# Projecting images 2 to 15 of a vision tower as two packed fp32r products instead of one fp32 product

## The chip, the cores and the metric

One core of one Trainium2 chip runs the whole kernel. The time is that of the device in microseconds, from several runs of the same program; the kernel before took 1002.57 us (median of 3 runs, 1000.47 to 1002.79). A further execution was taken with the hardware profiler: 1000.1 us, of which 998.5 us lie between the first and the last instruction. All rows of the trace are from that one.

## The reference, cut to what matters

Sixteen images of 256 tokens with 4 heads of 64 channels go through a token mixer, a gated recurrence with a residual, and a mixture of eight experts (top 2) with a shared expert. The change touches the first products:

```python
def proj(w, b):
    y = jnp.einsum('nclh,dc->ndlh', x, w) + b[None, :, None, None]
    return _flatten(y)
q, k, v = proj(Wq_w, Wq_b), proj(Wk_w, Wk_b), proj(Wv_w, Wv_b)
ek = jnp.exp(k)
num = jnp.einsum('ts,nsd->ntd', ew, ek * v)
den = jnp.einsum('ts,nsd->ntd', ew, ek)
y = jax.nn.sigmoid(q) * num / den
h = y @ out_w + out_b + _flatten(x)        # then layer norm, the recurrence, the experts
```

The host puts q, k, v and the residual with `out_b` side by side, so that one product with 256 columns per head gives all four.

## The kernel before

The kernel has two parts. The **mixer** takes the images one after another in a pipeline of steps t = 0 to 18: step t projects image t and forms its sums, works on the output, norm, gates and scan of image t-1, on the residual and norm of image t-2, and runs the shared expert and the routing for image t-3. Steps 0 to 3 and 16 to 18 are written out; steps 4 to 15 are a loop over pairs, whose body is `step` on each engine. The **experts** follow: 36 blocks of 256 routed rows.

Every engine runs its own written list of named pieces (`project0`, `hidden`, `gates0`, ...), and semaphores join them. Nothing is reordered at run time, so an engine that waits holds back all that stands behind it in its list. What the change and the steps of the prediction touch:

- TensorE: `project(n, par, lt)` makes one half (`lt`) of an image: four matmuls, one per head, with 128 tokens of x as the stationary operand (65 partitions: 64 channels and a row of ones for the bias; every fourth element, since the heads lie innermost) and 256 columns of `wproj` as the moving one, in fp32. In the trace each of these is two records of line 832, so eight records per half. The other large products already are fp32r with values split in a high and a low part: `split_product` (line 748) for `hidden`, `gates0/1`, `input0/1`, and `project_hidden` (line 764) for `ffn_out`.
- `project1` waits for `ekv0` of VectorE (the bank of PSUM is read by then), and `hidden(t, 0)` waits for `ekv1`, since it writes into the same banks.
- ScalarE: `exp_and_tanh` (lines 1299 to 1305) reads the projection three times; `copy_yt`, `copy_u`, `copy_v`, `gelu_j`, `high`, `tanh0/1` are the rest of its step.
- VectorE: `ekv` (1765), `h_sum`, `h_norm`, `u_stats`, `u_norm`, `v_sum`, `v_norm`, `ratio0/1` (reciprocals, 1772), `y_last`, `low` (the low parts for `ffn_out`, 1593), `gate_a/b`, the routing (`best`, `second`, `places`, `slots_out`), `base_sum` (1999).
- GpSimd: `inv_std` (517, 520) for three norms, `affine` (585, 587), `out_bias` (598), `rows_out` (four scattering DMAs, 524), and at two places the loading of a set of expert weights (`load_high`, `load_stage`, 4 MB) with the subtraction of its low parts (`split_low`, 510).
- SyncE: the loading of x, and the stores.
- Between the parts `block_limits` reads eight block limits on TensorE and ScalarE, and TensorE runs eight matmuls (line 1262) that produce nothing.

## Time and profile before

| what | us |
|---|---|
| median of 3 runs | 1002.57 |
| profiled execution | 1000.1 |
| its span | 998.5 |
| TensorE busy in it | 941.2 (94%) |
| VectorE, ScalarE, GpSimd busy | 676.5, 458.8, 380.1 |
| mixer, to the last product of the shared expert | about 543 |
| experts | about 445 |

Busy time of TensorE counts from a matmul's start to its modelled end; as matmuls overlap, the start-to-start distance is what one costs. The granted clock is given as a share of 2.4 GHz: 1.00 is 2.4 GHz throughout, 0.5 is 1.2 GHz. The mixer's steps are told apart by the transposes of Y with which each begins on TensorE (line 839): step 4 begins at 106.54 us and step 16 at 476.90 us.

### The profile page before, as it was taken

How to read it: one execution, taken by the hardware profiler on the slowest of the kernel's cores; microseconds unless marked ns; L12 is line 12 of the kernel's file. 1: busy time of each engine (PE TensorE's matmuls, PEld its weight loads, DVE VectorE, ACT ScalarE, POOL GpSimd, SP SyncE). 2: the span in 40 equal slices, each digit the busy share in tenths (PEclk: the TensorE clock that was granted, in tenths of full speed). 3: DMA queues.
4: the chain of work that ended last, by engine and by line, in shares of the span. 5: the costliest groups of instructions: out<-in, count | busy, mean ns of one | idle time of the engine just before them, and what ended most of it. 6: DMA issues, size and time to landing. Idle time of an engine off the chain costs nothing.

```text
span 998.5 us, 21487 instructions
## 1 busy us (share of the span) xinstructions
PE 941.2 (94%) x6801; PEld 879.6 (88%) x6801; DVE 676.5 (68%) x2092; ACT 458.8 (46%) x1132; POOL 380.1 (38%) x470
## 2 busy tenths in 40 slices
PE   6879999999999999999886999999999999999996
PEld 4667898888898888988786999999999999999995
DVE  3687878877888777788887365645656456554643
ACT  2214344444444434444332455555555555555553
POOL 5272533334324243233535334342423435342322
PEclk9989999999999999999999899999999999999998
DMA  9305111011110011100025727372463826474222
GB/s 271 134 18 168 43 43 37 17 32 42 42 42 16 26 42 42 42 21 11 33 95 195 202 47 204 55 216 43 101 157 50 215 47 145 117 174 92 43 43 32
DMA packets 49187, 84.84 MB, mean 85 GB/s; under 512 B 6415, under 2 KB 30881, under 8 KB 49154
## 3 DMA queue, kind: packets, MB, share of 16 engines
q0 software_dynamic: 31056, 57.46, 23.6%
q1 hardware_dynamic: 18098, 26.96, 9.2%
q8 instruction: 17, 0.28, 0.1%
q14 instruction: 16, 0.13, 0.0%
HBM read 55.34 MB, written 29.09 MB: 85 GB/s over the span
## 4 chain that ended last, share of the span: by engine, by line
PE 59%; issue 21%; POOL 9%; DVE 7%; ACT 1%; POOLq 1%; DMA 0%; DVEq 0%; SPq 0%; ACTq 0%
PE ps_nd L764 17%; PE ps_proj L748 13%; PE ps_ri L748 6%; PE ps_nd L925 6%; PE ps_proj L832 5%; POOL out L709 5%; PE ps_ip L748 4%; PE ps_h L913 2%; PE ps_t L839 2%; PE ps_ip L898 2%; PE ps_t L1234 1%; POOL v_rows L524 1%; DVE E L1765 1%; POOL rstd L520 1%; DVE yb L1999 1%
## 5 line engine op out<-in xcount | busy, mean ns | idle before, releaser
L1593 DVE TENSOR_TENSOR GL<-g_act,GH 128x256 fp32r<-128x256 f32 (+1 forms) x416 | 171.3, 425 | 166.4 <-ACT GH L1293 164.9
L1288 ACT ACTIVATE g_act<-ps_proj,fcb 128x256 f32<-128x256 f32 (+1 forms) x272 | 129.5, 476 | 277.9 <-PE ps_proj L748 253.4
L764 PE MATMUL ps_nd<-w2h,GH 128*128 128x256 f32 x832 | 240.6, 289 | 2.4 <-DVE GL L1593 2.2
L764 PE MATMUL ps_nd<-w2h,GL 128*128 128x256 f32 x832 | 233.8, 281 | 0.0
L764 PE MATMUL ps_nd<-w2l,GH 128*128 128x256 f32 x832 | 232.9, 280 | 0.0
L764 PEld LDWEIGHTS ps_nd<-w2h,GH 128*128 128x128 f32 x832 | 156.3, 188 | 6.9 <-issue 1.8
L1293 ACT CAST GH<-g_act 128x256 fp32r<-128x256 f32 (+1 forms) x416 | 161.0, 401 | 1.1
L764 PEld LDWEIGHTS ps_nd<-w2l,GH 128*128 128x128 f32 x832 | 157.0, 189 | 0.0
L764 PEld LDWEIGHTS ps_nd<-w2h,GL 128*128 128x128 f32 x832 | 156.4, 188 | 0.0
L748 PE MATMUL ps_proj<-xh,w1h 128*128 128x256 f32 (+1 forms) x544 | 126.8, 315 | 10.1 <-DVE E L1765 8.7
L709 POOL DMA_INDIRECT out<-yb,rows_to x72 | 115.6, 1605 | 16.7 <-issue 14.0
L748 PE MATMUL ps_proj<-xl,w1h 128*128 128x256 f32 (+1 forms) x544 | 111.8, 287 | 0.0
L748 PE MATMUL ps_proj<-xh,w1l 128*128 128x256 f32 (+1 forms) x544 | 111.3, 286 | 0.0
L748 PEld LDWEIGHTS ps_proj<-xh,w1h 128*128 128x128 f32 x544 | 86.7, 192 | 26.1 <-issue 14.3
L338 POOL TENSOR_TENSOR carrier_pool<-minus_half 1x1 f32<-1x1 f32 x48 | 10.9, 226 | 206.4 <-DVE slots L1987 113.9
L748 PEld LDWEIGHTS ps_proj<-xl,w1h 128*128 128x128 f32 x544 | 86.6, 194 | 0.0
L748 PEld LDWEIGHTS ps_proj<-xh,w1l 128*128 128x128 f32 x544 | 85.9, 193 | 0.0
L524 POOL DMA_INDIRECT v_rows<-v,slots x64 | 67.9, 1060 | 32.7 <-issue 16.6
L832 PE MATMUL ps_proj<-wproj,x 65*128 65x256 f32 x256 | 71.2, 425 | 6.8 <-DMA x<-x 6.2
L925 PE MATMUL ps_nd<-E,ewT 128*128 128x512 f32 x128 | 72.8, 702 | 2.8 <-DVE E L1765 2.8
L832 PEld LDWEIGHTS ps_proj<-wproj,x 65*128 65x128 f32 x256 | 64.1, 327 | 9.9 <-issue 7.9
L338 POOL TENSOR_TENSOR carrier_y<-minus_half 1x1 f32<-1x1 f32 x36 | 9.4, 261 | 162.8 <-DVE yb L2314 162.8
(266 smaller groups left out, 1829.9 us busy)
## 6 DMA issues: line engine op xcount, KB each, us to landing
R<-v_rows SPq DMA_DIRECT2D x37, 260.0 KB, 2.7
w1h<-fc_w POOLq DMA_DIRECT2D x9, 1024.0 KB
w2h<-pj_w POOLq DMA_DIRECT2D x9, 1024.0 KB
stage<-fc_w POOLq DMA_DIRECT2D x9, 1024.0 KB, 11.4
stage<-pj_w POOLq DMA_DIRECT2D x9, 1024.0 KB, 13.9
v_rows<-tail_rows SPq DMA_DIRECT2D x8, 520.0 KB, 4.5
x<-x SPq DMA_DIRECT2D x16, 256.0 KB, 3.5
out<-yb SPq DMA_DIRECT2D x16, 256.0 KB, 2.1
```

Of the source, the lines that this page charges most:

```text
L338: return pool.tensor_tensor(carrier[use][:], half, half, ALU.add)
L524: pool.indirect_dma_start(out=v_rows, out_offset=bass.IndirectOffsetOnAxis(ap=where_to, axis=0), in_=source, in_offset=None).then_inc(sema ...
L709: pool.indirect_dma_start(out=out, out_offset=bass.IndirectOffsetOnAxis(ap=rows_to[:, a:a + 1], axis=0), in_=yb[:, a, :], in_offset=None, ...
L748: last = pe.matmul(dst, w[a][:, k, cols], rhs, start=(q == 0), stop=(q == len(parts) - 1))
L764: last = pe.matmul(banks[a], g[:, j, a * P:(a + 1) * P], w[i][:, j, :], start=(j == 0 and q == 0), stop=(j == HT - 1 and q == 2))
L832: last = pe.matmul(ps_proj[:, h, :], head_view(par, lt, h), wproj[:, h, :], start=True, stop=True)
L839: last = pe.transpose(ps_t[:, f, lt * P:(lt + 1) * P], src[:, lt, f * P:(f + 1) * P], ident[:])
L898: last = pe.matmul(ps_ip[:, lt, :], HS[:, k, lt * P:(lt + 1) * P], wout_sb[:, k, :], start=(k == 0), stop=(k == FT - 1))
L925: last = pe.matmul(ps_nd[:, tt, :], ewT[:, s, tt * P:(tt + 1) * P], E[:, s, :], start=(s == 0), stop=(s == LT - 1))
L1288: act.activation(g_act[:, j % G_SLOTS, 0:width], banks[j % len(banks)][:, 0:width], ACT.Gelu_apprx_tanh, bias=fcb[i][:, j:j + 1]).then_inc ...
L1293: act.copy(GH[:, j, 0:width], g_act[:, j % G_SLOTS, 0:width]).then_inc(gh_done, 1)
L1593: dve.tensor_tensor(GL[:, j, 0:width], g_act[:, j % G_SLOTS, 0:width], GH[:, j, 0:width].bitcast(F32), ALU.subtract).then_inc(gl_done, 1)
```

## The change

For images 2 to 15, x is rounded to fp32r and taken apart. SyncE loads x twice, into partitions 0 to 63 and 64 to 127 of a wider `X`. ScalarE rounds both copies in one instruction (`x_high`, 128x1024) into `XA`, with the heads outermost, so that a head's tokens lie side by side. GpSimd subtracts (`x_low`, 64x1024) to give the low part in `XB`, which has 97 rows, with ones below. The weights are split too: `WA` holds the high part of the weights above the low part, `WB` the high part with the bias, zeros, and the low part of the bias. Two fp32r products per head, `XA` by `WA` and `XB` by `WB`, add up in one bank. Images 0 and 1 stay as they were.

```diff
-        X = [sb(f"x{i}", [KA, LH]) for i in range(2)]
+        X = [sb(f"x{i}", [P, LH]) for i in range(2)]
+        XA = [W1L[1][:].rearrange("p k n -> p (k n)")[:, i * LH:(i + 1) * LH] for i in range(2)]
+        XB = [W2L[1][:].rearrange("p j m -> p (j m)")[0:KB, i * LH:(i + 1) * LH] for i in range(2)]
+        WA = W1H[1][:, 0, :]
+        WB = W1H[1][0:KB, 1, :]
...
+                if packed:
+                    sp.dma_start(X[par][C:2 * C, :], x[n]).then_inc(x_loaded[par], 16)
...
+                    pool_wait(pool, xq_done, n - 1, "xq")
+                    pool.tensor_tensor(XB[p][0:C, :].rearrange("c (h l) -> c h l", h=H),
+                                       X[p][0:C, :].rearrange("c (l h) -> c h l", h=H),
+                                       XA[p][0:C, :].rearrange("c (h l) -> c h l", h=H).bitcast(F32),
+                                       ALU.subtract).then_inc(xs_done, 1)
...
+                    act.copy(XA[p].rearrange("c (h l) -> c h l", h=H),
+                             X[p][:].rearrange("c (l h) -> c h l", h=H)).then_inc(xq_done, 1)
...
+                        pe.matmul(ps_proj[:, h, :], packed_view(XA[par], lt, h), WA[:, cols],
+                                  start=True, stop=False)
+                        last = pe.matmul(ps_proj[:, h, :], packed_view(XB[par], lt, h),
+                                         WB[:, cols], start=False, stop=True)
...
             def next_weights(t, par):
+                pool.wait_ge(proj_ready, LT * NIMG)
                 load_high(pool, 1, 1)
                 load_stage(pool, 1)
...
+            def spare(t, par, k):
+                pe.wait_ge(consts, CONSTS)
+                for _ in range(2):
+                    pe.matmul(ps_ri[:, 1, :], ones_pp[:], zeros[:, 0, :], start=True, stop=True)
...
-            limits = block_limits(pe)
-            for _ in range(WARM):
-                pe.matmul(ps_t[:, 0, :], ones_r[:], W2H[0][:, 0, :], start=True, stop=True)
+            limits = [0] + block_limits(pe, 1, AHEAD)
             transpose_rows(0)
+            limits += block_limits(pe, AHEAD, NE + 1)
```

What else it does:

- The packed operands lie in the buffers of expert 1's weights. So `next_weights`, which before stood in step 2 of GpSimd's list, now stands in step 15 and waits until image 15 is projected; its subtractions follow in steps 15 and 18.
- The weights are packed in steps 0 and 1: two GpSimd copies of zeros and three DMAs (`pack_weights`), one VectorE subtraction of 65x1024 (`pack_split`), two more DMAs (`pack_lows`), and two ScalarE copies of ones (`pack_fill`).
- `x_high` stands in ScalarE's step after `copy_u` and `high(4)`; `x_low` in GpSimd's step between `rstd_v` and `out_bias`.
- All lists are in a new order. In TensorE's step the pieces now run `turn_y, project0, h_out, attention, project1, logits, hidden 0, hidden 1, sums0, hidden 2, hidden 3, sums1, hidden 4, hidden 5, turn_u, hidden 6, rank, hidden 7, gates0, turn_v, input0, gates1, ffn_out 0 to 2, input1, ffn_out 3 to 7`. In VectorE's step `ekv1` stands before `h_norm`, `low` 0 to 3 stand among the norms ahead of the reciprocals, and `y_last` comes later. Steps 14 and 15 are written out, with parts of step 15 drawn into step 14; the loop keeps steps 4 to 13. `low_first` and `low_second` of expert set 0 stand earlier on GpSimd.
- Eight `spare` pieces of two fp32 matmuls each stand in TensorE's steps 0 and 1, three of them ahead of the first projection.
- TensorE reads five of the eight block limits before the first transposes of the experts and three after; the eight idle matmuls go. ScalarE still reads all eight first.

## Rows read from the trace of the kernel before

**Rows 1.** The page: busy time and share of TensorE and its weight loads.

```profile
PE 941.2 (94%) x6801; PEld 879.6 (88%) x6801; DVE 676.5 (68%) x2092; ACT 458.8 (46%) x1132; POOL 380.1 (38%) x470
```

**Rows 2.** Busy time by stretch: length, PE, PEld, DVE, ACT, POOL, granted clock, DMA.

```profile
0.00:26.01 26.01, 16.55 (x36) 10.45 (x37) 9.89 (x19) 6.20 (x15) 13.15 (x33) 1.00 1.05 274
46.97:74.64 27.67, 21.89 (x97) 17.91 (x97) 22.54 (x43) 6.21 (x17) 19.94 (x19) 0.85 0.06 13
...
106.54:476.90 370.36, 361.64 (x2342) 325.67 (x2341) 298.63 (x970) 166.80 (x384) 136.98 (x173) 0.97 0.10 34
...
476.90:543.26 66.36, 56.96 (x436) 53.63 (x434) 56.13 (x196) 23.56 (x61) 32.09 (x30) 0.97 0.29 106
543.26:553.77 10.51, 2.92 (x12) 2.53 (x13) 3.77 (x16) 0.59 (x1) 0.55 (x1) 0.71 0.24 70
553.77:998.50 444.73, 434.34 (x3600) 430.14 (x3600) 247.42 (x740) 238.74 (x612) 163.95 (x199) 0.99 0.49 111
```

**Rows 3.** The same view for two successive steps of the loop, 6 and 7.

```profile
170.17:200.04 29.87, 29.19 (x197) 26.62 (x196) 24.58 (x81) 13.90 (x32) 11.21 (x14) 1.00 0.11 36
200.04:231.55 31.51, 30.83 (x197) 27.50 (x196) 24.71 (x81) 13.90 (x32) 11.20 (x14) 0.95 0.10 34
```

**Rows 4.** The critical chain through step 7: start, length, what.

```profile
200.65 1.97 PE ps_proj L832 x8
...
206.07 1.88 PE ps_proj L832 x8
...
208.93 0.44 DVE E L1765
...
213.75 0.72 PE ps_proj L748 x6
...
219.00 0.82 PE ps_proj L748 x6
```

**Rows 5.** TensorE's timeline in step 7, where it waits.

```profile
209.41 0.58 PE L748 MATMUL ps_proj<-xh,w1h 128*128 128x256 f32 x2 [0.68 <-DVE E L1765]
```

**Rows 6.** Groups by line: count, busy us, mean ns of one, idle before.

```profile
L1293 ACT CAST GH<-g_act 128x256 fp32r<-128x256 f32 x408 | 158.1, 401 | 1.1
...
L1407 ACT CAST gates_h<-TR 128x512 fp32r<-128x512 f32 x1 | 0.6, 641 | 0.0
...
L598 POOL TENSOR_TENSOR h<-h,bout_bc 128x512 f32<-128x512 f32 x16 | 20.6, 1286 | 12.1 <-DVE U L1616 12.1
...
L510 POOL TENSOR_TENSOR w1l<-stage,w1h 128x1024 fp32r<-128x1024 f32 x4 | 9.7, 2448 | 0.0
```

**Rows 7.** Timelines of GpSimd and VectorE where both are at work.

```profile
526.19 4.72 POOL L510 TENSOR_TENSOR w2l<-stage,w2h 128x1024 fp32r<-128x1024 f32 x2
...
526.20 5.26 DVE L1999 TENSOR_TENSOR yb<-yb,h 128x512 f32<-128x512 f32 x1
...
541.01 0.69 DVE L1999 TENSOR_TENSOR yb<-yb,h 128x512 f32<-128x512 f32 x1
```

**Rows 8.** Timelines of GpSimd and TensorE in the first 25 us.

```profile
3.76 0.12 POOL L549 IOTA lines_i<- 128x2 int32 x1
...
6.18 3.77 PE L832 MATMUL ps_proj<-wproj,x 65*128 65x256 f32 x8 [6.18 <-DMA x<-x]
...
16.85 6.21 PE L925 MATMUL ps_nd<-E,ewT 128*128 128x512 f32 x8 [1.56 <-DVE E L1765]
22.90 2.01 PE L832 MATMUL ps_proj<-wproj,x 65*128 65x256 f32 x8
```

**Rows 9.** Timelines of TensorE and VectorE in steps 1 to 3.

```profile
38.76 0.89 PE L839 MATMUL ps_t<-ident,U 128*128 128x128 f32 x4 [3.13 <-DVE U L1616]
...
65.53 0.66 PE L839 MATMUL ps_t<-ident,U 128*128 128x128 f32 x4 [2.95 <-DVE U L1616]
...
67.45 3.67 DVE L1616 TENSOR_SCALAR v<-h,mv,rstd 128x256 f32<-128x256 f32 x2
```

**Rows 10.** Stretch in which expert 1's four loads run, columns as rows 2.

```profile
72.00:87.00 15.00, 14.13 (x84) 12.57 (x83) 8.25 (x21) 7.03 (x15) 8.20 (x11) 0.85 0.96 288
```

**Rows 11.** The chain that ended last, between mixer and experts.

```profile
543.37 6.08 issue
549.45 2.07 PE ps_t L1262 x8
...
552.41 0.59 ACT xh L1572
...
553.03 0.70 DVE xl L2246
```

793 lines of the change are left out of this document (527 added, 266 removed).

## The prediction, made before the change was run

> **What bounds the kernel now.** I read the busy times first: TensorE is at work in 94% of the span, VectorE in 68% [rows 1]. That is an average, so I cut the span where the work changes [rows 2]. In the loop, steps 4 to 15, TensorE is busy 361.6 of 370.4 us; in the first 26 us it is busy 16.6, in the written-out end of the mixer 57.0 of 66.4, in the passage to the experts 2.9 of 10.5, and in the experts 434.3 of 444.7. So two thirds of a microsecond per step is all that TensorE is idle in the loop, and the view of single steps shows it twice: 29.19 of 29.87 us, 30.83 of 31.51 us [rows 3]. These two steps hold the same work, yet one is 1.64 us longer; its granted clock is 0.95 where the other's is 1.00, so in it TensorE ran for a while at 1.2 GHz instead of 2.4. This alternates through the loop, and the mean step is 370.36 / 12 = 30.86 us. The chain through a step [rows 4] is almost all TensorE: it leaves it once, after `project1`, for ScalarE's reads and VectorE's `ekv1` (the 0.44 us row of line 1765), and comes back at `hidden(t, 0)` after 0.68 us of idleness [rows 5]. Whatever shortens TensorE's list in the loop shortens the loop, until another engine's list is as long. VectorE's is next: 24.6 us of work in a step, against 13.9 for ScalarE and 11.2 for GpSimd [rows 3].
>
> **The change part by part, on TensorE in the loop.** It removes two fp32 halves per image: 1.97 and 1.88 us on the chain [rows 4]. It adds two halves of eight fp32r matmuls with 256 columns. The same shape stands in the chain as `hidden`: six in 0.72 us, or 0.82 us where a small product stands before them [rows 4]. Per matmul that is 0.12 us, so eight take 0.96 us, and 1.06 with the dearer beginning. A step saves 1.97 + 1.88 - 0.96 - 1.06 = 1.83 us. The row is that of a 128-row stationary operand; XA has 128 rows and XB 97, and both are contiguous, so I see no reason for a dearer one. The bounds are 1.5 (if each half still begins 0.15 us later than I count) and 1.95. The wait before `hidden(t, 0)` stays as it is: it runs from the end of `project1` through ScalarE and VectorE, and none of its members changes; moving `ekv1` ahead of `h_norm` gains nothing while VectorE waits there anyway.
>
> **The same, on the other engines in the loop.** `x_high` on ScalarE: 256 elements take 401 ns and 512 take 641 ns [rows 6], 240 ns per further 256, so 1024 take an estimated 1.12 us. No row shows a read of every fourth element on ScalarE; bounds 1.1 and 2.2 us (twice), of which I take the lower end, because the rows nearest to it are the same instruction. ScalarE's step grows from 13.9 to 15.0 us, which lies beside TensorE's 28. Behind `x_high` in the queue stands `tanh0`, then `high(5)` and `copy_v`; `tanh0` waits for `gates0`, which comes some 2 us later, so the 1.1 us is covered. `x_low` on GpSimd: 1024 elements take 2.45 us [rows 6], by length and not by partitions, bounds 2.4 and 4.9 us (twice, for the strided read). GpSimd goes from 11.2 to 13.7 us plus a small carrier operation. Behind `x_low` stand `out_bias` (first wanted by `v_sum` of the next step) and `rows_out`, which waits for `slots_out` late in the step anyway. The second DMA of x is 256 KB on a DMA that is 10% busy [rows 2]; x is loaded most of a step ahead. All of that costs nothing on TensorE's path.
>
> What is not free is where GpSimd and VectorE meet. While GpSimd subtracts two pieces of weights, a VectorE addition that takes 0.69 us alone takes 5.26 us and ends with GpSimd's second piece [rows 7]. So such an operation, with both inputs in SBUF, is held until GpSimd is through, even across two GpSimd instructions. `x_low` with `out_bias` behind it is such a pair in every step: 2.45 + 1.29 = 3.7 us at most. VectorE's `low` and `y_last` are operations of this kind; the reciprocals, which read PSUM, are not. By my count along the new lists, `x_high` ends some 17.7 us into the step and `x_low` runs from there to about 20.3, when VectorE is at `ratio0` and `ratio1` (17 to 21 us). So mostly cover, some 0.5 us of holding in an average step. VectorE has 24.6 us of work and a new step of 28.0 or more, and since its waits do not all shrink, part of this will now and then reach `ffn_out` 6 and 7. I charge 0.35 us per step for this and for the new order; bounds 0 and 0.8.
>
> The Trainium skill (page "SBUF — State Buffer", section "Who interferes with whom") says that a VectorE instruction with two SBUF inputs contends with a GpSimd instruction that reads SBUF, and that one fully blocks; the trace agrees (5.26 for 0.69 us). A second rule speaks against the change: "GPSIMD Engine Reference", section "Performance pitfalls for Q7 kernels", puts reads with a step over 8 bytes at about 2.9 cycles per element in place of 1.9. No row here shows it; by it `x_low`, with its step of 16 bytes, would take an estimated 3.7 us instead of 2.45, still within my bounds.
>
> **Loop and steps 14, 15.** 12 x (1.83 - 0.35) = 17.8 us; bounds 12 x 0.8 = 10 and 12 x 1.95 = 23. The granted clock may change with the step's length: it cost 1.64 us in every second step. None at all gives 10 us more, in every step 10 us less; as the list around the wait stays the same, I keep one in two and give it 5 us to both sides.
>
> **Steps 0 to 3.** Constants are there at 3.9 us, x at 6.2 [rows 8]. Three spares are six fp32 matmuls of 256 columns, each about a quarter of a half-projection's 3.77 us, so 0.9 us and 5.6 us together: the first projection starts at some 9.5 instead of 6.2. But all work up to 22 us ran at half speed: a half-projection took 3.77 us against 2.01 later, the sums 6.21 [rows 8] against 3.7. If the earlier work brings the clock up by about 9 us, that saves 1.8 + 1.8 + 2.5 = 6.1 us, less the 3.3 of delay: -3 (bounds +3 and -5). Images 2 and 3 are packed: -3.7, of which TensorE's waits for u (3.13 and 2.95 us [rows 9]) may eat some; I take -3. The subtraction of expert 0's low parts moves ahead, and with it goes the time in which v's norm was held (3.67 us for two operations that need 0.74 [rows 9]); stretch 46.97 to 74.64 has 5.8 us idle and a clock of 0.85 [rows 2]. I take -3 (bounds 0 and -7). Packing the weights adds 1.4 us to VectorE before `u_norm`, on that image's chain, and work on GpSimd and ScalarE in stretches in which they have nothing to do; I take +0.5. Together -8.5, bounds 0 and -14.
>
> **The end of the mixer.** The 66.4 us have 9.4 us of idleness [rows 2], and the new order pulls work of later steps forward: I take -3, bounds -7 and +8. The upper bound is the late weights: the four loads of expert 1 kept the DMA at 0.96 for 15 us [rows 10]. They now start after the last projection, and GpSimd waits for them in `next_low_first`, then subtracts for 4.7 us [rows 7]; behind it stand `rows_out(15)`, `out_bias(15)` and `rstd_h(16)`. From the last projection that makes 20 us, then some 7 for the scatters and `out_bias`; a step lasts 28, so `rstd_h(16)` is reached just as image 15's sums come.
>
> **The passage.** Reading eight limits takes 6.08 us, 0.76 each, then eight idle matmuls 2.07, then transposes, xh and xl [rows 11]. With five limits first, the transposes wait for the rows, which land at about 548.5; ScalarE still reads all eight, until some 549.6. xh then starts at 549.7 instead of 552.4: -2.6, bounds -4 and +1 (a longer time at 1.2 GHz without the idle matmuls). **The experts** keep their 444.7 us, within 1.
>
> Sum: -17.8 - 8.5 - 3 - 2.6 = -31.9. The profiled execution's 1000.1 us would become 968.2; the median stood 2.5 us higher, so the forecast is 1002.6 - 31.9 = 970.7, say 970 us.
>
> **The rivals.**
> - *VectorE becomes the pace, and half comes back.* For it: 24.6 us of work, some 5.3 of waits per step, and the holding. If its round takes 29.3 us instead of TensorE's 28.2 before clock, the loop gains 0.4 us per step: 5 instead of 17.8, so 983. Against it: `low` 0 to 3 now fill the waits for the norms. Chance 0.17.
> - *Slower: VectorE is held in every step.* If `x_low` slides by 3 us (ScalarE's list late), it meets `low` 4, 5 and `y_last`, not the reciprocals. Then a round is 24.6 + 3.7 held + 5.3 of waits = 33.6 us against 30.86 now: 12 x 2.7 = +33, with -14 elsewhere 1021. It decides from where VectorE's round passes 30.86 + 14 / 12 = 32.0 us, that is, if it keeps all its waits and is held over 2.1 us. Chance 0.06.
> - *The weights come late.* If the loads take 25 us beside the scatters instead of 15, GpSimd hands out image 14's and 15's norms some 8 us late, and the end of the mixer takes that once: 981. Chance 0.1.
> - *The packed product isn't cheaper.* If TensorE ran each fp32r half at the fp32 half's pace, only start and passage would gain: 992. Against it, all `hidden` rows. Chance 0.02.
>
> **How the numbers follow.** The forecast has 0.65; its own range, from the bounds taken together without all ends at once, is 957 to 982. 8 in 10 need most of the two rivals at 981 and 983 as well: 955 to 988. About 0.3% (3 us) is what a measurement can tell from no change. Faster by more: 0.65 + 0.17 + 0.1 and half of the last rival's 0.02, which makes 0.93; within: the other half, 0.01, since the start's bounds reach +3; slower: 0.06.
>
> **What would show it.** Eight fp32r records where line 832's eight fp32 records stood, in 0.96 to 1.06 us a half, show the first step. Steps of 28.0 to 28.5 us at a clock of 1.00 show that TensorE still sets the pace; steps over 29 with waits of TensorE for GL would show VectorE. `x_low` in GpSimd's timeline gives its 2.45 us, and VectorE operations of over 1 us beside it show holding. The first projection at 9 to 10 us with halves of under 2 us shows the start; the first expert product 2 to 3 us nearer to the mixer's last shows the passage. The forecast is wrong if TensorE shows idle stretches over 1 us per step or at the weights' subtraction.

## The result and the profile after

The changed kernel takes 1005.99 us (median of 20 runs, 1000.11 to 1011.26) against 1001.0 us for the kernel before beside it: a ratio of 1.0053, 95% interval 1.0038 to 1.0069. It is slower by half a per cent, where 970 us and "faster" were forecast. The profiled execution took 1005.59 us with a span of 1004.0, against 1000.1 and 998.5.

Busy time by stretch of the changed kernel (length, PE, PEld, DVE, ACT, POOL, granted clock, DMA share, GB/s). The first four are steps 0 to 3, the fifth is the loop; each begins with the transposes of Y, as in rows 2:

```profile
0.00:27.82 27.82, 20.89 (x65) 15.71 (x66) 9.68 (x18) 5.26 (x12) 15.95 (x38) 0.94 1.00 263
27.82:49.97 22.15, 17.82 (x84) 11.84 (x82) 18.07 (x46) 7.63 (x18) 15.13 (x12) 0.85 0.86 221
49.97:86.25 36.28, 21.67 (x104) 17.26 (x105) 27.93 (x43) 8.93 (x19) 15.19 (x14) 0.81 0.00 1
86.25:116.92 30.67, 27.91 (x199) 24.88 (x198) 25.38 (x74) 14.20 (x31) 6.47 (x9) 1.00 0.00 1
116.92:414.89 297.97, 277.16 (x1953) 249.55 (x1951) 272.01 (x802) 161.26 (x330) 151.40 (x164) 0.99 0.15 45
414.89:552.73 137.84, 122.26 (x824) 111.34 (x824) 111.32 (x349) 52.25 (x126) 63.07 (x65) 0.91 0.31 104
552.73:558.61 5.88, 0.66 (x5) 0.42 (x4) 3.58 (x15) 0.59 (x1) 0.00 (x0) 0.90 0.03 10
558.61:1004.00 445.39, 435.04 (x3600) 430.81 (x3600) 247.59 (x740) 239.35 (x612) 164.46 (x199) 0.99 0.49 111
```

The sixth of these covers steps 14, 15 and the mixer's end, because the change writes steps 14 and 15 out and reorders them. The same work in the kernel before is this stretch:

```profile
415.77:543.26 127.49, 116.73 (x826) 107.83 (x824) 105.43 (x356) 51.37 (x125) 54.25 (x58) 0.97 0.20 70
```

The ledger, with the starts of steps 4 and 14 at 106.54 and 415.77 in the kernel before:

| stretch | before | after | difference | forecast |
|---|---|---|---|---|
| steps 0 to 3 | 106.5 | 116.9 | +10.4 | -8.5 |
| steps 4 to 13 | 309.2 | 298.0 | -11.3 | -14.8 (10 of the 12 steps of -17.8) |
| steps 14, 15 and the end | 127.5 | 137.8 | +10.4 | -6.0 (the other two, and -3) |
| passage | 10.5 | 5.9 | -4.6 | -2.6 |
| experts | 444.7 | 445.4 | +0.7 | 0 |

The two kernels are told apart here by one profiled execution each. How far such a stretch varies with the same code shows in the traces of the experiments below. In the five kernels with the changed kernel's order of steps 0 to 3, itself among them, step 4 began at 116.6 to 120.7 us. From step 14 to the first expert product (143.7 us in the changed kernel, 138.0 before), the ten kernels with its order there took 139.3 to 146.0 us. So the signs in the ledger hold, and the two differences of 10.4 us are good to a few us.

The loop did win, but the two stretches ahead of and behind it, which run once each, took back nearly twice that. In the loop TensorE is now busy 277.2 of 298.0 us, 27.7 of 29.8 per step, where it was busy all but 0.7 us of each step. The wait is new. The clock is at 0.99: of the stretches at 1.2 GHz that stood in every second step [rows 3], and cost 1.64 us each, one is left, in step 4.

The packed product does what it says. The chain through the beginning of one half of it (start, length, what):

```profile
184.54 0.12 PE ps_proj L909
184.65 0.12 PE ps_proj L911
184.77 0.12 PE ps_proj L909
```

Eight such pieces make a half of 0.97 us, where rows 4 have 1.88 and 1.97. What stands beside it in a step does not do as forecast. Timeline of ScalarE, GpSimd, VectorE and TensorE in a step (start, length, engine, line, operation; in brackets the idle time before it and who ended it):

```profile
196.28 2.07 ACT L1572 CAST w1l<-x 128x1024 fp32r<-128x1024 f32 x1
198.57 2.91 POOL L659 TENSOR_TENSOR w2l<-x,w1l 64x1024 fp32r<-64x1024 f32 x1
201.45 1.47 POOL L618 TENSOR_TENSOR h<-h,bout_bc 128x512 f32<-128x512 f32 x1
200.60 2.61 DVE L1821 TENSOR_TENSOR GL<-g_act,GH 128x256 fp32r<-128x256 f32 x2
208.86 0.63 PE L921 MATMUL ps_t<-ident,Y 128*128 128x128 f32 x4 [1.24 <-DVE xl L2054]
```

`x_high` takes 2.07 us instead of 1.12, `x_low` 2.91 instead of 2.45, and it ends 0.8 us after VectorE's `ratio1`. `low` 4 and 5, about 0.4 us each elsewhere, take 2.61 together: `low` 4 ends when `x_low` has ended, and `low` 5 when `out_bias` has. At the step's end TensorE waits 1.24 us with `turn_y` for `v_low` (1.15 to 1.32 in the loop's steps), besides the old 0.68.

Ahead of the loop, GpSimd's `x_low(2)`, `low_second(2)` and `out_bias(2)` stand in a row, v's norm is held beside them, and TensorE waits for what follows from it:

```profile
69.10 2.85 POOL L659 TENSOR_TENSOR w2l<-x,w1l 64x1024 fp32r<-64x1024 f32 x1
71.93 4.63 POOL L530 TENSOR_TENSOR w2l<-stage,w2h 128x1024 fp32r<-128x1024 f32 x2
76.52 1.30 POOL L618 TENSOR_TENSOR h<-h,bout_bc 128x512 f32<-128x512 f32 x1
69.17 8.80 DVE L1844 TENSOR_SCALAR v<-h,mv,rstd 128x256 f32<-128x256 f32 x2 [0.58 <-POOL rstd L540]
78.72 1.09 PE L921 MATMUL ps_t<-ident,v 128*128 128x128 f32 x4 [7.70 <-DVE UTL L2034]
```

Rows 9 had 3.67 us for the same two operations of the norm. Here the first of them alone takes 7.53 us, until `low_second` is through, and the second 1.35, until `out_bias` is. (The section on the change says that `low_second` of set 0 stands earlier. Only `low_first` does; `low_second(2)` kept its place behind `rstd_v(2)`, and `x_low(2)` was put directly ahead of it.)

Behind the loop TensorE waits 3.62 us ahead of `project0(15)` and 3.87 us ahead of `attention(16)`. From step 14 to the first expert product the granted clock is at half, that is 1.2 GHz, for 25.1 us, where before it was for 13.0.

```profile
443.20 4.63 DVE L1821 TENSOR_TENSOR GL<-g_act,GH 128x256 fp32r<-128x256 f32 x1
448.55 0.55 PE L909 MATMUL ps_proj<-w1h,w1l 128*128 128x256 f32 x1 [3.62 <-ACT g_act L1444]
474.01 4.94 POOL L530 TENSOR_TENSOR w1l<-stage,w1h 128x1024 fp32r<-128x1024 f32 x2 [9.37 <-DMA stage<-pj_w]
490.82 2.50 PE L980 MATMUL ps_ip<-wout_sb,HS 128*128 128x256 f32 x5 [3.87 <-DVE HS L2086]
```

### The profile page after: what moved, and what is told of

Same layout as the page of the kernel before. It is cut to its first block, busy times and chain, and to the rows that moved or that the text cites. A ratio compares the mean times of both kernels' runs of the same rounds, so it can differ in the third digit from the quotient of the medians.

```text
span 1004.0 us, 21462 instructions
## 1 busy us (share of the span) xinstructions
PE 923.4 (92%) x6825; PEld 861.8 (86%) x6825; DVE 715.5 (71%) x2081; ACT 489.5 (49%) x1148; POOL 431.7 (43%) x499
## 3 DMA queue, kind: packets, MB, share of 16 engines
q1 hardware_dynamic: 19218, 30.64, 10.4%
## 4 chain that ended last, share of the span: by engine, by line
PE 39%; issue 24%; DVE 19%; POOL 12%; ACT 2%; DMA 2%; POOLq 1%; ACTq 0%; DVEq 0%; SPq 0%
PE ps_nd L829 11%; PE ps_proj L813 9%; POOL out L774 5%; DVE GL L1821 4%; DVE rden L2000 4%; PE ps_ri L813 3%; PE ps_nd L1007 3%; PE ps_ip L813 3%; PE ps_h L995 2%; PE ps_ip L980 2%; DMA stage<-pj_w 1%; DVE v L1844 1%; PE ps_proj L909 1%; PE ps_proj L911 1%; PE ps_t L921 1%
## 5 line engine op out<-in xcount | busy, mean ns | idle before, releaser
L1821 DVE TENSOR_TENSOR GL<-g_act,GH 128x256 fp32r<-128x256 f32 (+1 forms) x416 | 199.2, 489 | 174.0 <-ACT GH L1449 154.0
L829 PE MATMUL ps_nd<-w2h,GH 128*128 128x256 f32 x832 | 244.0, 293 | 3.1 <-DVE GL L1821 3.1
L813 PE MATMUL ps_proj<-xh,w1h 128*128 128x256 f32 (+1 forms) x544 | 124.1, 310 | 8.5 <-DVE E L1993 6.8
L774 POOL DMA_INDIRECT out<-yb,rows_to x72 | 116.0, 1611 | 16.8 <-issue 13.5
L544 POOL DMA_INDIRECT v_rows<-v,slots x64 | 70.0, 1094 | 32.5 <-issue 16.7
L1007 PE MATMUL ps_nd<-E,ewT 128*128 128x512 f32 x128 | 63.6, 623 | 3.0 <-ACT ewT L1548 1.6
L537 POOL TENSOR_TENSOR ve<-mv,eps 128x2 f32<-128x2 f32 x48 | 11.8, 245 | 117.1 <-DVE mv L1841 117.1
L2000 DVE RECIPROCAL rden<-ps_nd 128x256 f32<-128x256 f32 x32 | 55.9, 1747 | 3.8 <-PE ps_nd L1007 3.8
```

The costliest lines, as they stand in the source:

```text
L544: pool.indirect_dma_start(out=v_rows, out_offset=bass.IndirectOffsetOnAxis(ap=where_to, axis=0), in_=source, in_offset=None).then_inc(sema ...
L774: pool.indirect_dma_start(out=out, out_offset=bass.IndirectOffsetOnAxis(ap=rows_to[:, a:a + 1], axis=0), in_=yb[:, a, :], in_offset=None, ...
L813: last = pe.matmul(dst, w[a][:, k, cols], rhs, start=(q == 0), stop=(q == len(parts) - 1))
L829: last = pe.matmul(banks[a], g[:, j, a * P:(a + 1) * P], w[i][:, j, :], start=(j == 0 and q == 0), stop=(j == HT - 1 and q == 2))
L1007: last = pe.matmul(ps_nd[:, tt, :], ewT[:, s, tt * P:(tt + 1) * P], E[:, s, :], start=(s == 0), stop=(s == LT - 1))
L1821: dve.tensor_tensor(GL[:, j, 0:width], g_act[:, j % G_SLOTS, 0:width], GH[:, j, 0:width].bitcast(F32), ALU.subtract).then_inc(gl_done, 1)
```

## The experiments

Each ratio is against runs of the kernel before on the same chip (medians of 1001.0 to 1001.5 us). "Start" is the beginning of step 4, "loop" steps 4 to 13, "end" from step 14 to the first expert product (137.84 + 5.88 = 143.7 us in the changed kernel), all from one profiled execution each. For the whole time the medians count.

### First: the order in the loop, the layout of x, the product, the spares

**e1_vlow_first.**

```diff
                 low(t, par, 7)
-                gate_a(t, par)
                 v_low(t, par)
+                gate_a(t, par)
```

> One change in VectorE's order inside the loop (steps 4 to 13): v_low stands ahead of gate_a instead of behind it, so that turn_y of the next step, which waits for v_low, can begin sooner. Theory A (VectorE's list sets the step since the change: TensorE's wait of 1.15 to 1.32 us at each step's start is v_low's place alone): the wait falls under 0.3 us and half or more of it is kept, steps 4 to 13 go from 29.4 to 28.2 to 28.9 us each, the whole 5 to 12 us shorter than the changed kernel, at 994 to 1001 us. Rival B (VectorE is full: what leaves turn_y comes back at gates or hidden 0, because x_low's 2.9 us and out_bias hold VectorE for 2 us in every step): the wait moves, the step stays within 0.2 us of 29.4, the whole within 2 us of 1006.

Measured: 998.47 us, ratio 0.9973 (0.9955 to 0.9990). The loop took 288.4 us, 28.5 a step from the second on; the wait at `turn_y` is gone. One line moved takes 7.5 us off the changed kernel. Theory A holds, although `low` 4 and 5 are held as before (VectorE is busy 26.7 us of such a step): the order decides what the hold reaches.

**e2_unstrided.**

```diff
-  act.copy(XA[p].rearrange("c (h l) -> c h l", h=H), X[p][:].rearrange("c (l h) -> c h l", h=H))
+  act.copy(XA[p], X[p][:])
-  return buf[:, h * L + lt * P:h * L + (lt + 1) * P]
+  return buf.rearrange("c (l h) -> c l h", h=H)[:, lt * P:(lt + 1) * P, h]
```

and `x_low` likewise.

> ScalarE's copy of x and GpSimd's subtraction go through x in the order in which it lies, and TensorE picks every fourth value when it loads the packed halves, as it did for the fp32 product. Theory A (reading at a step of four values is what made x_high 2.07 us instead of the forecast 1.12, and x_low 2.91 instead of 2.45, and x_low's length is what holds VectorE's low 4): x_high takes 1.1 to 1.2 us, x_low 2.4 to 2.5, the held low 4 loses 0.4 us or more, each loop step 0.2 to 0.6 us, the whole 3 to 7 us less than the changed kernel, 999 to 1003 us. Rival B (the length is set by something else, the wider copy or the rounding on write): x_high stays near 2.0 and the time within 1 us of 1006. Rival C (TensorE pays for the step: its eight packed instructions of 0.12 us become longer by what it saved): projection halves of 1.5 us or more and a whole of 1010 or more.

Measured: 1012.76 us, ratio 1.0115 (1.0095 to 1.0135). A and C are both true, and C is the larger. The groups of ScalarE's and GpSimd's passes (count, busy us, mean ns), the changed kernel's first and then this one's:

```profile
L1572 ACT CAST w1l<-x 128x1024 fp32r<-128x1024 f32 x10 | 20.6, 2063 | 0.0
L659 POOL TENSOR_TENSOR w2l<-x,w1l 64x1024 fp32r<-64x1024 f32 x11 | 32.1, 2917 | 11.1 <-ACT w1l L1572 11.1
```

```profile
L1570 ACT CAST w1l<-x 128x1024 fp32r<-128x1024 f32 x10 | 10.5, 1051 | 0.0
L659 POOL TENSOR_TENSOR w2l<-x,w1l 64x1024 fp32r<-64x1024 f32 x10 | 23.9, 2387 | 0.0
```

The forecast's 1.12 and 2.45 us were right for a read in a row; the step of four values doubles ScalarE's pass and adds 22% to GpSimd's. With the shorter passes the wait at `turn_y` is gone here too. But TensorE pays. Weight loads of one projection line (ns min/median/max) and the chain through two of its matmuls: this kernel; then the loads of the changed one, and of the one before.

```profile
L907 PEld LDWEIGHTS ps_proj<-w1h,w1l x8: 309/330/330, 206.9 to 213.5; 128*128 128x128 f32 x8
207.18 0.24 PE ps_proj L907
207.41 0.23 PE ps_proj L909
```

```profile
L909 PEld LDWEIGHTS ps_proj<-w1h,w1l x6: 190/190/193, 209.2 to 213.9; 128*128 128x128 f32 x6
```

```profile
L832 PEld LDWEIGHTS ps_proj<-wproj,x x16: 309/329/329, 200.4 to 207.3; 65*128 65x128 f32 x16
```

A load that takes every fourth value takes 330 ns against 190, and the matmuls then follow each other at 0.23 us: as fast, or as slow, as the fp32 product did at the same step. The packed product from x as it lies saves nothing: the loop took 308.4 us, before 309.2. What pays in this change is the copy that puts each head's values in a row, together with fp32r; the price is ScalarE's 2.07 us.

**e3_fp32_product.** The fp32 product from x in all images, in the changed kernel's orders and beside all its new passes. The projection's constant row is left out of images 2 to 15.

```diff
-  pe.matmul(ps_proj[:, h, :], packed_view(XA[par], lt, h), WA[:, cols], start=True, stop=False)
-  last = pe.matmul(ps_proj[:, h, :], packed_view(XB[par], lt, h), WB[:, cols], ...)
+  last = pe.matmul(ps_proj[:, h, :], head_view(par, lt, h), wproj[:, h, :], ...)
```

> The changed kernel with the packed product alone taken back: all images use the fp32 product from x and the fp32 weights, while x_high, x_low, the packing and every order stay as they are. The row of ones in x is overwritten by the second load, so the projection's constant row is left out of images 2 to 15; the work is the same in size. It prices the packed product within the new orders. Theory A (the product's gain of 1.85 us a step is real, but part of it only made TensorE wait 1.2 us for VectorE at the step's start): steps 4 to 13 go from 29.4 to 30.2 to 31.0 us, the whole to 1013 to 1024 us. Rival B (TensorE is wholly masked by VectorE in the loop): steps stay at 29.4 to 29.8 and the whole rises by 6 us or less. Rival C (nothing masked): 31.2 us a step or more, over 1026 us.

Measured: 1055.88 us, ratio 1.0540 (1.0507 to 1.0573). Some 12 us of this are the experts' stage (457.4 us instead of 445.4, with 3700 matmul records instead of 3600, so one block more: without the constant row the rows go to the experts in other numbers). The loop took 321.4 us, 23.4 more than in the changed kernel: ten times 1.83, and for the rest four stretches at 1.2 GHz where the changed kernel has one. Rival C: nothing was masked. And this says more than the number. TensorE's wait at `turn_y` in this kernel:

```profile
220.96 0.63 PE L915 MATMUL ps_t<-ident,Y 128*128 128x128 f32 x4 [1.25 <-DVE xl L2048]
```

The step is some 1.85 us longer (31.1 to 31.5 us against 29.2 to 29.6, where the clock is 1.00) and the wait is the same 1.25. Had VectorE's whole round been the pace, a longer step would have swallowed it. So the wait is made within the step, behind the projection, by a chain from `x_high` over `x_low` to `v_low`. That VectorE is full, as rival B of e1 had it, falls.

**e4_no_spares.** All eight `spare(...)` lines taken out.

> The changed kernel without its eight spare products in steps 0 and 1 (six instructions of three of them stand ahead of the first projection, which begins at 10.5 us instead of 6.2). Theory A (the spares ahead of the first projection put 2 to 4 us on the path through the cold start, and those ahead of turn_y up to 1.8 us): first projection at 6.0 to 6.5 us, y(0) turned at 25 to 27, the whole 2 to 5 us less than the changed kernel, 1001 to 1004. Rival B (what the spares cost in place they give back in clock: with them TensorE's granted clock is full from 11.3 us on, before only from 22): first projections cold at 3.9 us each, step 2 starts at 50 us or later, and the time is the same or up to 3 us more.

Measured: 1005.89 us, ratio 1.0039 (1.0024 to 1.0055): the changed kernel's time. The first projection starts at 6.13 us but takes 3.77; with the spares it starts at 10.48 and takes 2.39. Timeline of the changed kernel's start:

```profile
5.20 5.49 PE L1108 MATMUL ps_ri<-zeros,ones_pp 128*128 128x256 f32 x12 [5.20 <-DMA wproj<-w_proj]
10.48 2.39 PE L914 MATMUL ps_proj<-wproj,x 65*128 65x256 f32 x8
14.44 2.21 PE L914 MATMUL ps_proj<-wproj,x 65*128 65x256 f32 x8 [0.17 <-DVE E L1993]
```

Both reach y(0) at 27.5 to 27.8 us. Rival B: place and clock cancel. (The trace's record of the clock begins at 11.3 us with the spares and at 22.6 without them; what lies ahead of it is counted as 1.00 in the rows by stretch, so that there the lower level shows in the lengths, 3.77 us against 2.01 for the same half later.)

### Second: what the passes of GpSimd hold

**e12_quarter_low.** The changed kernel, and `x_low` in the loop over a quarter of the columns; the other low halves are left out.

```diff
-  XB[p][0:C, :].rearrange("c (h l) -> c h l", h=H)
+  XB[p][0:C, :].rearrange("c (h l) -> c h l", h=H)[:, :, 0:L // 4]
```

> Base is the changed kernel itself (1006 us), its order untouched. In the loop x_low subtracts a quarter of the columns of each head (64 x 256 values instead of 64 x 1024); the other low halves are left as an earlier image had them, so that part of the computation is left out. It is a dose of the hold alone. Theory A (x_low's 2.91 us beside VectorE holds low 4 and low 5 by 1.9 us, VectorE works without a gap from there to v_low, so the hold is what makes TensorE wait 1.15 to 1.3 us at turn_y): x_low about 0.8 us, low 4 and 5 at 0.42 us each, the wait under 0.3 us, steps 4 to 13 at 28.2 to 28.6 us instead of 29.4, the whole 994 to 999 us. Rival B (the wait comes from copy_v and turn_v, or from gate_a's place alone; VectorE would only have an earlier gap): the wait stays over 0.8 us and the time within 2 us of 1006.

Measured: 989.44 us, ratio 0.9895 (0.9855 to 0.9935). The loop took 281.25 us, with steps of 27.9 and no wait of TensorE but the old 0.68. GpSimd in this kernel:

```profile
197.67 0.85 POOL L660 TENSOR_TENSOR w2l<-x,w1l 64x256 fp32r<-64x256 f32 x1
198.49 1.28 POOL L618 TENSOR_TENSOR h<-h,bout_bc 128x512 f32<-128x512 f32 x1
```

Theory A, and more than it asked: over ten steps the loop is 16.7 us shorter. A settled step is 1.55 us shorter (27.87 for 29.42), and step 4 is 2.7 shorter, in which the changed kernel also has its one stretch at 1.2 GHz. The forecast charged 0.35 us a step. Three quarters of `x_low` are gone here and not all of it, so this is the hold's price at least.

**e5_low_second_early**, on e1's order.

```diff
             affine(2, 0)
+            low_second(2, 0)
             rstd_u(2, 0)
             rstd_v(2, 0)
             x_low(2, 0)
-            low_second(2, 0)
             out_bias(2, 0)
```

> v_low ahead of gate_a as in e1_vlow_first (998.5 us), and besides low_second(2) moved up on GpSimd, from behind x_low(2) to behind affine(2), so that no long pass runs beside v_norm(2), which took 7.5 us behind x_low (2.85) and low_second (4.63). Theory A (those two passes back to back hold v_norm and so cost TensorE's idle 7.7 us ahead of turn_v): v_norm falls to 0.7 to 3 us, the idle ahead of turn_v to under 4 us, step 4 starts 3 to 5 us sooner and the whole is 994 to 996 us. Rival B (the pass only moves the hold: it now holds u_stats, gate_b or v_sum of step 2, and the stretch is unchanged): step 4 starts within 1 us of where it did, 997.5 to 999.5 us.

Measured: 991.81 us, ratio 0.9912 (0.9885 to 0.9938), 6.7 us less than e1 by the medians. Start at 110.4 us instead of 116.6; over all traces, the ten kernels with this order of the start reach step 4 at 113.4 us on average (110.4 to 119.2), the five with the changed kernel's at 119.0. The rows of VectorE and TensorE:

```profile
68.71 4.21 DVE L1844 TENSOR_SCALAR v<-h,mv,rstd 128x256 f32<-128x256 f32 x2 [0.26 <-POOL rstd L540]
73.67 0.63 PE L921 MATMUL ps_t<-ident,v 128*128 128x128 f32 x4 [2.78 <-DVE UTL L2034]
```

Theory A, with more than its 994 to 996 us, though the norm fell only to 4.21 us and not under 3: it is still held, now by `x_low` and `out_bias` (2.85 + 1.3 us).

**e7_step_on_write**, on e1's order: x read in a row, XA and XB written at a step of 256 values.

```diff
-  act.copy(XA[p].rearrange("c (h l) -> c h l", h=H), X[p][:].rearrange("c (l h) -> c h l", h=H))
+  act.copy(XA[p].rearrange("c (h l) -> c l h", h=H), X[p][:].rearrange("c (l h) -> c l h", h=H))
```

> v_low ahead of gate_a as in e1_vlow_first (998.5 us), and besides x_high and x_low go through x in the order in which it lies and write at a step of 256 values, instead of reading at a step of 4 and writing in a row. The result in memory is the same, so TensorE's loads are as in the changed kernel. It asks which side of the step costs ScalarE 2.07 instead of 1.05 us and GpSimd 2.91 instead of 2.39. Theory A (the step on reading costs, and one on writing doesn't): x_high 1.1 us, x_low 2.4 us, the held low 4 at most 0.9 us as in e2_unstrided, and the whole 2 to 5 us less, 993.5 to 996.5. Rival B (either step costs the same): 2.0 and 2.9 us, the time within 1 us of 998.5. Rival C (writing at so wide a step costs more): x_high over 2.5 us and the whole 1 to 6 us more.

Measured: 998.35 us, ratio 0.9976 (0.9959 to 0.9994); `x_high` 2.07 us, `x_low` 2.95. Rival B. For ScalarE, whose one input is now read in a row, it shows that the step costs the same on either side. For GpSimd it doesn't separate the two, since `x_low` now reads XA at a step of 256 values too.

### Third: the mixer's end

**e6_split_later** and **e8_stage_early**, on e1's order.

```diff
-                load_stage(pool, 1)         # e8, in next_weights
 ...
             out_bias(3, 1)
+            load_stage(pool, 1)             # e8
 ...
-            next_low_first(17, 1)           # e6, e8
             rows_out(15, 1)
 ...
             rows_out(17, 1)
+            next_low_first(17, 1)           # e6, e8
             next_low_second(18, 0)
```

> v_low ahead of gate_a as in e1_vlow_first (998.5 us), and besides the first half of the split of expert 1's weights moved from ahead of rows_out(15) to behind rows_out(17), just ahead of the second half. The weights arrive as late as before; only nothing on GpSimd waits for them in step 15 any more. Theory A (the late weights cost the mixer's end its 11 us, because rstd_h(16), whose turn comes behind the transfer, the 4.97 us of the split, four scatters and a pass, is late, and TensorE idles 3.87 us ahead of attention and more behind it): the mixer ends 5 to 9 us sooner, the whole at 989 to 994 us. Rival B (the end's price is the order itself: the cold clock and the waits of step 15 and 16 stand as they are, and both splits in a row, 9.5 us, now hold yb and the last rows): the whole within 2 us of 998.5.

> As e6_split_later, and besides the two transfers of expert 1's staged weights issued in step 3, since only the rounded halves need the memory that the packing occupies. Three sizes of one cause, with e1_vlow_first and e6_split_later: how much of the mixer's end is the late weights. Theory A: the late issue is two DMAs (1.7 us on GpSimd) and half the bytes shorter, worth 0 to 2 us more than e6_split_later, at 988 to 993 us. Rival B (the early transfers' own issue in step 3 or their traffic costs as much as it saves): within 1 us of e6_split_later.

Measured: 1003.52 us (1.0018, interval 1.0005 to 1.0031) and 1005.08 us (1.0040, 1.0023 to 1.0056). Both are slower than e1, and theory A falls in both. The end took 150.9 and 150.5 us, where e1 had 146.0. The wait ahead of `attention(16)` stands although `rstd_h(16)` no longer waits for any transfer, so the late weights don't make it. And a 2.0 us wait ahead of a rank product grows to 6.61: VectorE's `base_sum`, 0.69 us alone [rows 7], is held for 7.87 beside the two splits in a row:

```profile
484.97 3.78 PE L980 MATMUL ps_ip<-wout_sb,HS 128*128 128x256 f32 x8 [3.62 <-DVE HS L2086]
527.52 7.87 DVE L2227 TENSOR_TENSOR yb<-yb,h 128x512 f32<-128x512 f32 x1
525.49 4.73 POOL L530 TENSOR_TENSOR w1l<-stage,w1h 128x1024 fp32r<-128x1024 f32 x2
530.16 4.67 POOL L530 TENSOR_TENSOR w2l<-stage,w2h 128x1024 fp32r<-128x1024 f32 x2
```

**e9_first_half_in_16, e10_scan_first, e11_both_late**, all on e5.

```diff
-            next_low_first(17, 1)       # e9, e11
             rows_out(15, 1)
 ...
             rows_out(16, 0)
+            next_low_first(17, 1)       # e9, e11
 ...
             ekv1(16, 0)
+            gate_b(15, 1)               # e10, e11
             best(16, 0)
             h_norm(16, 0)
-            gate_b(15, 1)               # e10, e11
```

> Base is e5_low_second_early (991.8 us: v_low ahead of gate_a, low_second(2) behind affine(2)). Besides, the first half of the split of expert 1's weights goes from ahead of rows_out(15) to behind rows_out(16), where GpSimd is idle for 18 us (489.5 to 507.7 in that kernel); the second half stays. Theory A (the late weights cost something where they block GpSimd: rows_out(15), out_bias(15) and rstd_h(16) wait for the transfer that ends at 459.1 and the 4.94 us of splitting): from step 14's start to expert 1's first product 1 to 3 us less than the base's 143.7, the whole 988.5 to 991 us. Rival B (TensorE's wait of 3.8 us ahead of attention(16) is VectorE's order, gate_b behind best and h_norm, as it stayed at 3.62 us in e6_split_later, and the split beside VectorE's work of step 16 costs as much there): within 1 us of the base or up to 2 us more.

> Base is e5_low_second_early (991.8 us). Besides, gate_b(15) with its scan stands ahead of best(16) and h_norm(16) on VectorE instead of behind them. Theory A (TensorE's wait of 3.84 us ahead of attention(16) is made by the order on VectorE: the scan waits behind 1.6 us of best and the wait for rstd_h): the wait falls to 1.5 us or less, and 1.5 to 2.5 us of it are kept: whole 989.3 to 990.5 us. Rival B (what is put off comes late in turn: h_norm later, so u_norm, turn_u and gates0(16) later by the 2.7 us of gate_b): the wait moves to turn_u, the whole within 1 us of 991.8.

> Both edits of e9_first_half_in_16 and e10_scan_first on the same base. With the first half out of the way rstd_h(16) can be ready sooner, and the scan is no longer behind it. If the two waits are independent, the gains add up (theory A: 986.5 to 990 us); if one only uncovers the other, it equals the better of the two; rival B: 990.8 to 993.

Measured: e9 998.58 us (0.9974, 0.9959 to 0.9989), e10 992.71 (0.9915, 0.9893 to 0.9937), e11 998.93 (0.9974, 0.9956 to 0.9991), against e5's 991.81. e9 lost 7 us, by this:

```profile
489.23 4.70 POOL L530 TENSOR_TENSOR w1l<-stage,w1h 128x1024 fp32r<-128x1024 f32 x2
488.53 5.44 DVE L1963 TENSOR_SCALAR rmask_z<-rhit,ident 128x16 fp32r<-128x16 f32 x1
497.94 0.58 PE L829 MATMUL ps_nd<-w2h,GH 128*128 128x256 f32 x1 [6.17 <-DVE GL L1821]
```

A VectorE operation on 16 values a partition, which takes 0.23 us in e6, is held for 5.44 us. It starts 0.7 us ahead of the split, beside the issue of a scatter (488.24, 0.96 us), and ends with the split. TensorE waits 6.17 us behind it, and the granted clock is at half for 10.2 us from 495.3 on. In e10 the wait ahead of `attention(16)` is gone, and 2.53 us stand ahead of a rank product and 1.71 ahead of the class row's. That is rival B in kind, though the wait didn't move to `turn_u` (0.28): nothing is left in the time. e11 adds e9's loss to e10's nothing.

**e15_low14_sooner** and **e16_passage_back**, on e5.

```diff
             rstd_v(14, 0)
+            x_low(14, 0)                # e15
             rows_out(14, 0)
             out_bias(14, 0)
-            x_low(14, 0)                # e15
 ...
-            limits = [0] + block_limits(pe, 1, AHEAD)                 # e16
-            transpose_rows(0)
-            limits += block_limits(pe, AHEAD, NE + 1)
+            limits = [0] + block_limits(pe, 1, NE + 1)
+            for _ in range(8):
+                pe.matmul(ps_t[:, 0, :], ones_r[:], W2H[0][:, 0, :], start=True, stop=True)
+            transpose_rows(0)
```

> Base is e5_low_second_early. x_low(14), written out behind the loop, stands directly behind rstd_v(14) on GpSimd instead of behind rows_out(14) and out_bias(14). In the base a low of VectorE is held for 4.6 us at that place (out_bias and x_low back to back), and TensorE waits 3.6 us ahead of project0(15). Theory A (that hold and that wait are one thing): the low at under 1.5 us, the wait under 1 us, 2 to 4 us less in all, 988 to 990 us. Rival B (project0(15) waits for the last gelu of image 11 by its place in ScalarE's list): the wait stays near 3.6 us and the time within 1 us of 991.8.

> Base is e5_low_second_early. The passage from mixer to experts on TensorE is as before the change: all 8 limits are read ahead of the first transposes, with the 8 warming products between. It prices the split of the limits alone. Theory A (reading the limits costs TensorE about 0.75 us each; with 3 of 8 behind the transposes and no warming products it won 4.6 us in the trace of the change, less what ScalarE's 8 limits keep): 2 to 4.5 us more, 993.8 to 996.3 us. Rival B (ScalarE's own reading of the 8 limits sets the passage either way): within 1 us of 991.8.

Measured: e15 992.85 us (0.9922, 0.9902 to 0.9942), e16 998.16 (0.9950, 0.9930 to 0.9971). In e15 the 3.6 us wait ahead of `project0(15)` became 0.81, as theory A has it, but v's norm of step 14 is now held (3.3 us for 0.7) and TensorE waits 2.5 at `turn_v`: nothing is left in the time. e16 costs 6.4 us by the medians, more than theory A's 2 to 4.5. Its trace shares that out: step 4 began at 115.8 us, e5's at 110.4, in the same code, and the passage itself is 9.75 us (544.66 to 554.41) against 6.25. So the limits and the idle matmuls are worth 3.5 us, theory A, and the rest is scatter of the start and the end. The rows, chain of e16:

```profile
544.66 5.42 issue
550.08 2.07 PE ps_t L1419 x8
```

### Fourth: where out_bias stands, and x in two pieces

Four kernels on e5. The edits are the place of `out_bias` in the loop, and `x_high` and `x_low` in two instructions of two heads each, so that GpSimd begins 1 us sooner:

```diff
                 rstd_v(t, par)
+                out_bias(t, par)        # e13, e14
                 x_low(t, par)
-                out_bias(t, par)        # e13, e14, e17
                 rows_out(t, par)
+                out_bias(t, par)        # e17
 ...
+  for q in range(2):                    # e14, e17, e18, and x_low likewise
+      hs = slice(q * H // 2, (q + 1) * H // 2)
+      act.copy(XA[p].rearrange("c (h l) -> c h l", h=H)[:, hs],
+               X[p][:].rearrange("c (l h) -> c h l", h=H)[:, hs]).then_inc(xq_done, 1)
```

> Base is e5_low_second_early (991.8 us; loop step 28.5). In the loop out_bias stands ahead of x_low on GpSimd instead of directly behind it. In the base the trace shows low 4 at 1.10 us while x_low ends and low 5 at 1.51 us while out_bias runs, against 0.42. Theory A (two passes back to back hold VectorE through both; with out_bias gone from there low 5 runs free and out_bias costs less beside the passes of u_norm and low 1): low 5 at 0.42 us, the step 27.9 to 28.4, the whole 3 to 6 us less, 986 to 989 us. Rival B (out_bias now holds low 1, v_norm or low 3 by as much): step within 0.1 us of 28.5 and the whole within 1 us of 991.8.

> As e13_bias_first, and besides x_high and x_low work in two pieces of two heads each, so that GpSimd starts about 1 us sooner, while VectorE is busy with the reciprocals of ratio0 and ratio1, which read PSUM and weren't held in any run. Theory A (what is left of the hold is 0.7 us at low 4): no held low at all, the loop step at 27.8 to 28.1 us as in e12_quarter_low (27.9 with TensorE's only wait 0.68), the whole 984 to 987 us. Rival B (the four shorter instructions cost more in all, or the first piece now holds u_low or low 3): no better than e13_bias_first within 1 us.

> Base is e5_low_second_early (991.8 us, step 28.5), with x_high and x_low in two pieces each and nothing else; out_bias stays directly behind x_low. With e13 and e14 it makes a table of two edits. Theory A (the hold is the time from the end of ratio1 to the end of GpSimd's passes in a row, x_low and out_bias together; starting 1 us sooner takes 1 us off it): the held lows lose about 1 us, the step is 27.9 to 28.2 us and the whole 986 to 989 us. Rival B (the first piece meets low 3 or v_norm and holds them by as much): step within 0.1 us of 28.5, the whole within 1 us of 991.8.

> Base is e14_two_pieces (989.4 us), with out_bias in the loop behind rows_out instead of ahead of x_low: no pass stands directly behind x_low, and none beside u_low, where e13 and e14 show a new wait of 0.5 to 0.66 us ahead of gates0. Theory A (each pass of GpSimd costs what VectorE has to do beside it that needs the shared way to SBUF; at the step's end there is less of it): no wait at gates0 and no held low, step 27.9 to 28.2, the whole 984 to 988 us. Rival B (out_bias comes so late that v_sum or h_sum of the next step waits or is held): step 28.6 or more, the whole 989 to 996 us.

| kernel | x in | out_bias | time, us | ratio, 95% | usual step |
|---|---|---|---|---|---|
| e5 | one piece | behind x_low | 991.81 | 0.9912 (0.9885 to 0.9938) | 28.5 |
| e13 | one piece | ahead of x_low | 991.06 | 0.9903 (0.9867 to 0.9938) | 28.7 |
| e14 | two pieces | ahead of x_low | 989.42 | 0.9874 (0.9857 to 0.9890) | 28.7 |
| e18 | two pieces | behind x_low | 984.50 | 0.9826 (0.9810 to 0.9843) | 28.0 |
| e17 | two pieces | behind rows_out | 980.28 | 0.9789 (0.9772 to 0.9806) | 27.86 |

e5, e13 and e14 can't be told apart by their times, whose intervals overlap; e18 and e17 are clear of them and of each other. In e13 and e14 `low` 4 and 5 run free, but `out_bias` now holds `low` 2 (1.51 us, in the pair's 1.84), `u_low` comes late, and TensorE waits for it ahead of `gates0` in every step. That is rival B for e13, and the two pieces of e14 gain nothing in the step.

```profile
193.49 1.84 DVE L1827 TENSOR_TENSOR GL<-g_act,GH 128x256 fp32r<-128x256 f32 x2
196.97 0.50 PE L816 MATMUL ps_ri<-UTH,gates_h 128*128 128x256 f32 x2 [0.64 <-DVE UTL L2040]
```

In e18 the pair `low` 4 and 5 still takes 2.03 us instead of 2.61, and TensorE no longer waits behind it. In e17 the pair runs all but free (0.85), since GpSimd's second piece ends at 192.11, just after VectorE is through with its reciprocals. `out_bias`, at the step's end, now holds `base_sum` (1.31 us for 0.69), and TensorE doesn't wait for that:

```profile
188.90 1.56 POOL L661 TENSOR_TENSOR w2l<-x,w1l 64x512 fp32r<-64x512 f32 x1
190.57 1.54 POOL L661 TENSOR_TENSOR w2l<-x,w1l 64x512 fp32r<-64x512 f32 x1
189.95 1.75 DVE L2006 RECIPROCAL rden<-ps_nd 128x256 f32<-128x256 f32 x1
191.89 0.85 DVE L1827 TENSOR_TENSOR GL<-g_act,GH 128x256 fp32r<-128x256 f32 x2
201.25 1.31 DVE L2233 TENSOR_TENSOR yb<-yb,h 128x512 f32<-128x512 f32 x1
```

Both came out under their expected times (986 to 989 and 984 to 988 us), e18 by 1.5 and e17 by 3.7, with the steps as expected: the surplus of e17 isn't in the loop. e17 beats both kernels: 2.1% under the one before (interval 1.9 to 2.3), with the same packed product and the same sums; three places in the order and the cut in two differ from the change. Its loop took 280.6 us (before 309.2), TensorE's idle time in it is 8.1 us, and the clock is 1.00.

## Why the prediction was wrong, step by step

**Where the miss lies.** Between the forecast's -31.9 us and the traces' +5.5 are 37.4 us. By the ledger 18.9 of them are steps 0 to 3, 16.4 the end, 3.5 the loop and 0.7 the experts; the passage came out 2.0 better. The loop's sum is within its bounds even so (-11.3 in ten steps; -13.5 in twelve, bounds -10 and -23), but not by its terms: the hold cost 13 us more than was charged, and the clock, of which the forecast said that it could go either way, gave back half of that. That is luck. The step that failed is the price of GpSimd's passes beside VectorE. In the loop it was charged at 0.35 us a step, where e12 shows 1.55 to 1.67. At v's norm of step 2 it was taken to go away, 3 us to the good, and the norm was held for 8.8 us. With most of these holds taken away by order and by cutting two passes in two, and all the work kept, the kernel takes 980.3 us (e17), inside the forecast's range of 957 to 982. For the end's part of the miss the cause stays open.

**The terms.** *The packed half on TensorE* was right: 0.97 us a half, forecast as 0.96 and 1.06, and e3's steps are some 1.85 us longer. The reason given for it was incomplete. It read the price off `hidden`'s rows and noted that XA and XB lie in a row. e2 shows that this word carried the whole gain, since from x as it lies the packed half costs what the fp32 half cost.

*x_high* is the first term that was mis-sized. The bounds were 1.1 and 2.2 us, twice for the unseen step; I took the lower end because the nearest rows were the same instruction. They were the same instruction without the step, and the step was what had no row. It measured 2.07. Then I costed it at nothing because TensorE was busy beside it. Its real price is that it hands x to GpSimd a microsecond later; e18, in which GpSimd begins 1 us sooner, has steps of 28.0 us where e5 has 28.5.

*x_low* is the second: 2.91 us for 2.45 (2.39 without the step, in e2). The rule of the Trainium skill ("GPSIMD Engine Reference", "Performance pitfalls for Q7 kernels", about 2.9 cycles per element in place of 1.9), by which I had estimated 3.7 us, has the sign right. The size is 22% here, not 50; one of this subtraction's two inputs is read at the step. There is a rule that I did not weigh. The Trainium skill, page "Advanced Engine Details and Errata", section "Memory Cachelines", says that SBUF has lines of 16 bytes and that a different line at every access costs. x at every fourth fp32 value is such a read. The page gives no size; the runs agree in kind for ScalarE (2.06 for 1.05 us), TensorE's weight loads (330 for 190 ns) and GpSimd (2.92 for 2.39).

*The hold* is the term that failed in the loop. The forecast had the mechanism, its two instructions and the sum of 3.7 us at most, and let all but 0.5 us of it fall on reciprocals, with 0.35 us charged. `x_low` was put at 17.7 to 20.3 us into the step; it ran from 19.1 to 22.0 (198.57 in a step that began at 179.45), then `out_bias` to 23.5, and VectorE was through with `ratio1` at 21.2. Two mis-sized terms of 1.0 and 0.5 us moved the pair past the reciprocals' end. e12 prices it at 1.55 us per settled step, against bounds of 0 and 0.8, and at 16.7 us over the ten steps; the whole fell by 16.5. e17 comes to the same step (27.86 us) with the whole subtraction kept. (The loop's lower bound was added up wrongly, too: 1.5 - 0.8 is 0.7 a step, so 8 us and not 10.)

*The clock* gave more than was kept: one stretch at 1.2 GHz in ten steps where there were five, some 7 us for the better. With 18.3 for the product that makes 25, and TensorE is busy 24.7 us less (277.2 for 301.9). Its idle time grew by 13.4 us: ten waits at `turn_y` make 12.3, one in step 4, for `x_low` ahead of `project0`, makes 1.8, and elsewhere it lost 0.7. Less work and more idleness together are the loop's -11.3. Why the five stretches went no run separates; e12 and e17, with steps of 27.9 us, have none in the loop, e2, with the product at the old price, has seven.

*Steps 0 to 3* (-8.5 forecast, +10.4): step by step they are 1.8, 1.2 and 8.6 us longer and, in step 3, 1.2 shorter than before, so it is step 2. The sign failed at the sentence by which the subtraction moves ahead and the time goes in which v's norm was held. Of the two subtractions only `low_first` had moved. The one beside the norm, `low_second(2)`, stood where it had stood, and `x_low(2)` had been put directly ahead of it. The norm grew from 3.67 to 8.8 us, and e5 gets 6.2 us back in the start by moving one line (5.6 by the averages). The spares were forecast at -3 and are worth 0 (e4). Packing the weights, forecast at 1.4 us on VectorE, took 2.89, in step 1. Even e5's start is 4 us behind the kernel before; what of the forecast's other terms, the packed images above all, is missing in it no run separates.

*The end* (-6 forecast with steps 14 and 15, +10.4 measured, past the upper bound): the bound's reason was the late weights, and it isn't borne out. They are late (the transfer ends 13.1 us after its issue, GpSimd waits 9.37), but in e6 and e9 nothing waits for them, and the wait ahead of `attention(16)` stands in e6 and the end is longer in both. Their own price stays unmeasured, since in both the moved split holds VectorE elsewhere. What the two rows of that stretch show is TensorE busy for 5.5 us longer, although its two packed images save 3.7, at a clock of 0.91 for 0.97, and 4.8 us more of idleness (15.6 for 10.8). The clock goes with the waits: the waits of 3.6, 3.9 and 3.5 us end at 448.6, 490.8 and 556.2 us, and stretches at 1.2 GHz begin at 448.2, 489.2 and 557.4. So such a wait costs more than its length. The length of one wait isn't the whole rule: three further such stretches follow waits of 0.8 to 2.0 us, while the loop's waits of 1.25 were followed by none. What makes the end's waits stays open: e15 shows that GpSimd's two passes in a row made the one of 3.6 and e10 that VectorE's order made the one of 3.9, but both got as much back elsewhere.

*The passage* was right in kind and under-sized: -4.6 for -2.6, past the bound of -4 by 0.6. e16 measures 3.5 us for the limits and the idle matmuls. ScalarE's reading of its 8 limits is the new chain there, as forecast. *The experts*: +0.7, within 1.

**The rivals.** "Slower: VectorE is held in every step" was the one that came true in kind, with 0.06; its place was right (`low` 4 and 5), its price of 2.7 us a step was too high by a us, and the point from which it decides was put wrongly. The slower time that it names, 1021 us, was not reached, because the start and the end, and not the loop, made the kernel slower. It was made to depend on VectorE's whole round passing 32.0 us. e3 shows that the round has nothing to do with it: a chain inside the step, `x_high`, `x_low`, `low`, `gate_a`, `v_low`, `turn_y`, sets the wait whatever the step's length. "VectorE becomes the pace" falls for the same reason. "The weights come late" put the price of an 8 us delay on the end once; the end did grow, but not for that wait (e6). "Not cheaper" falls with the chain rows, and e2 shows how near it was.

**The chances.** 0.93 for faster rested on four negative terms. The one term with rows of its own kind, the product, held, and so did the sign of the passage. The start and the end were sums over moves that left out what runs beside them on the other engines, and no rival had either of them losing time by its order.

## What to carry to other kernels

Where a GpSimd pass is added, lay its start and end, worked out with the dearer bound, against VectorE's list, and then do the same with the pass behind it. That one holds either the same VectorE operation on (v's norm, 7.53 us through three instructions) or the next one (`low` 5, 1.51 us). Here 4.4 us of passes cost TensorE 1.55 us a step, and cost it nothing once they began 1 us sooner and no longer stood in a row.

Ask of every wait whether it shrinks when the step gets longer by a known amount elsewhere. If it doesn't, it is a chain inside the step, and the place of one line can remove it (`v_low`: 7.5 us).

An fp32 operand that is read at a step of 16 bytes cost more on each of the three engines that read it so. In this kernel it paid to let ScalarE do that once, ahead of the product.

And judge a part of the kernel that runs once from more than one trace: with the same code, step 4 began between 110.4 and 119.2 us.

## What the runs showed of the hardware

- Weight loads of 128 columns at a step of four fp32 values take 330 ns (e2, and the kernel before), in a row 190 (the changed kernel). A matmul record of 256 columns then follows the last one at 0.23 us in fp32 and fp32r alike. In a row it follows at 0.12 (fp32r) or 0.22 (fp32, lines 980 and 995: eight in 1.73). So the step costs the fp32r product half its speed and the fp32 one hardly anything.
- ScalarE's pass over 128x1024 fp32 takes 1.05 us in a row (e2) and 2.07 at a step of 16 bytes in reading (the changed kernel) or of 1024 bytes in writing (e7). GpSimd's over 64x1024 takes 2.39 us in a row, 2.92 with one input at a step of 16 bytes, and 2.95 with the other input and the output at one of 1024.
- It isn't only operations with two tensors as input that GpSimd holds: a `TENSOR_SCALAR`, with one tensor from SBUF to SBUF, is held as well (v's norm, two of them, 8.80 us for 0.7; `rmask_z`, 5.44 for 0.23). The Trainium skill, page "Advanced Engine Details and Errata", section "VectorE Performance Modes", names a mode for input and output in SBUF that reads through two ports, and says that GpSimd shares the second one and that the two block each other. The rows agree in that these operations are held. Whether they run in that mode no row shows: one of the norm's two takes 0.40 us for 256 values, as long as `low` with its two inputs. Operations that read PSUM ran at their usual length beside GpSimd (the reciprocal 1.75 us, the sum of `ps_nd` in e6 0.42 us).
- One VectorE operation can be held through several GpSimd instructions in a row (three in the changed kernel's step 2, 7.53 us; four in e6, 7.87 us), or slip in between two of them (`low` 4 and 5, and the norm before, 1.32 and 2.43 us under the two halves of `low_second`).
